# Causal attention by four heads and one query block instead of two heads and one or two query blocks: key ring, order of maxima, transposed gather

## What is computed

```python
x = x + 0.5 * ffn(layernorm(x))
x = x + attention(layernorm(x))
x = x + 0.5 * ffn(layernorm(x))
# ffn: weights of 4-bit codes times a scale per 32, H = 256, MLP_DIM = 2048
gate, up = xt @ Wg.T, xt @ Wu.T
out = (gelu_tanh(gate) * up) @ Wd.T
# attention, N_HEAD = 16, hd = 16
scores = einsum('bqhd,bkhd->bhqk', q, k) / sqrt(hd)
scores = where(causal, scores, finfo.min)
o = einsum('bhqk,bkhd->bqhd', softmax(scores), v)
return o @ Wo.T + bo
```

## Time and profile before

| | us |
|---|---|
| median of 3 runs (1113.87 to 1118.17) | 1116.4 |
| profiled execution, own time | 1118.69 |
| its span, first to last instruction | 1117.0 |
| attention, first score to last `weigh` | 351.8 to 829.3 |
| TensorE busy in the span | 1071.8 |
| VectorE busy | 699.0 |
| ScalarE busy | 577.9 |
| GpSimd busy | 112.6 |
| mean granted TensorE clock | 0.994 of 2.4 GHz |

### The profile page before, as it was taken

How to read it: one execution, slowest core, us unless ns; L and a number is a source line. 1 busy time by engine, 2 the same in 40 slices (tenths; PEclk the granted TensorE clock), 3 DMA queues, 4 the chain that set the end, 5 groups by cost and what they waited for, 6 DMA issues and landing times.

```text
span 1117.0 us, 17563 instructions
## 1 busy us (share of the span) xinstructions
PE 1071.8 (96%) x6448; PEld 707.1 (63%) x6448; DVE 699.0 (63%) x1620; ACT 577.9 (52%) x1107; POOL 112.6 (10%) x409
## 2 busy tenths in 40 slices
PE   4999999998999989999999999999999999999998
PEld 3888888887876533333333333333349888888887
DVE  5986545446556487888888888888544434344333
ACT  4764443342344656666777776777663333333322
POOL 1000000000001136331111111111100000000000
PEclk9999999998999899999999999999999999999999
DMA  6001040060030732322022202200000000000000
GB/s 195 2 1 47 7 126 1 11 175 16 10 123 1 202 65 55 67 53 53 14 41 54 53 1 54 53 1 2 1 1 1 1 20 1 1 19 1 20 1 19
DMA packets 75223, 43.81 MB, mean 39 GB/s; under 512 B 47161, under 2 KB 68993, under 8 KB 75137
## 3 DMA queue, kind: packets, MB, share of 16 engines
q1 hardware_dynamic: 75137, 42.68, 15.7%
HBM read 25.63 MB, written 16.78 MB: 38 GB/s over the span
## 4 chain that ended last, share of the span: by engine, by line
PE 87%; DVE 6%; ACT 2%; issue 2%; DMA 1%; SPq 0%; POOL 0%; ACTq 0%; DVEq 0%; POOLq 0%
PE psum L850 16%; PE psum L635 14%; PE psum L782 12%; PE psum L723 11%; PE psum L738 10%; PE psum L867 8%; PE psum L650 8%; DVE attn_part_max L1327 2%; PE psum L792 2%; PE psum L682 2%; ACT attn_prob L1141 1%; PE psum L826 1%; PE psum L694 1%; PE psum L124 1%; DVE attn_junk L1330 1%
## 5 line engine op out<-in xcount | busy, mean ns | idle before, releaser
L1141 ACT ACTIVATE attn_prob<-psum 128x512 f32<-128x512 f32 (+3 forms) x640 | 301.2, 540 | 145.7 <-PE psum L723 142.0
L1327 DVE TENSOR_REDUCE attn_part_max<-psum 128x1 f32<-128x512 f32 x384 | 243.7, 684 | 50.1 <-PE psum L738 48.2
L635 PE MATMUL psum<-ffn_xt,all_w_hi 128*128 128x512 f32 x512 | 166.0, 406 | 0.0
L782 PE MATMUL psum<-attn_prob,attn_vals 128*32 128x512 f32 (+3 forms) x1280 | 156.9, 544 | 0.1
L1330 DVE CUSTOM_DVE_ANT_0 attn_junk<-psum,attn_mask 128x128 bf16<-128x128 f32 (+3 forms) x256 | 116.9, 485 | 24.9 <-PE psum L738 24.4
L1432 DVE TENSOR_TENSOR ffn_act_out<-ffn_act_out,psum 128x512 f32<-128x512 f32 x64 | 44.0, 688 | 109.3 <-ACT ffn_act_out L1177 109.2
L650 PE MATMUL psum<-all_w_hi,ffn_inner 128*128 128x256 f32 x512 | 105.0, 288 | 0.1
L1177 ACT ACTIVATE ffn_act_out<-psum 128x512 f32<-128x512 f32 x64 | 38.2, 597 | 127.3 <-PE psum L850 127.3
L635 PEld LDWEIGHTS psum<-ffn_xt,all_w_hi 128*128 128x128 f32 x512 | 92.7, 192 | 16.4 <-issue 0.3
L867 PE MATMUL psum<-all_w_hi,ffn_inner 128*128 128x256 f32 x512 | 102.5, 283 | 0.1
L635 PE MATMUL psum<-ffn_xt,all_w_lo 128*128 128x512 f32 x256 | 100.7, 393 | 0.0
(11 more groups left out here) (150 smaller groups left out, 1674.2 us busy)
## 6 DMA issues: line engine op xcount, KB each, us to landing
qk_rows<-qkv_parts SPq DMA_DIRECT2D x16, 384.0 KB, 2.5
qk_rows<-qkv_parts SPq DMA_DIRECT2D x16, 256.0 KB, 2.9
attn_q_early<-qk_rows SPq DMA_DIRECT2D x8, 384.0 KB, 4.5
attn_q_late<-qk_rows SPq DMA_DIRECT2D x8, 384.0 KB, 3.7
attn_k_mid<-qk_rows SPq DMA_DIRECT2D x3, 768.0 KB, 6.7
attn_k_late<-qk_rows SPq DMA_DIRECT2D x3, 768.0 KB, 7.3
all_x<-in_L_attn_h SPq DMA_DIRECT2D x4, 512.0 KB, 6.7
v_rows<-qkv_rows_v SPq DMA_DIRECT2D x16, 128.0 KB, 2.5
```

The costliest lines, as they stand in the source:

```text
L635: last = nc.tensor.matmul(psum[:, 2 * m + q % 2, :], w_part[a][:, 3 * g + m, pl, o:o + P], xt[:, b % 2, c, pl, :], start=(n == 0), stop=(n ...
L782: last = nc.tensor.matmul(psum[r:r + 32, O0, at:BT], vals[:, k0 * SUB + kb + k, 2 * hd:2 * hd + 32], prob[:, (4 * d + 2 * k + hd) % PRING, ...
L1141: nc.scalar.activation(prob[:, n % PRING, at:BT], psum[:, S0 + n % SBANKS, at:BT], ACT.Exp).then_inc(s["exp"], 1)
L1327: nc.vector.tensor_reduce(to, psum[:, bank, :], AX.X, ALU.max).then_inc(s["max_read"], 1)
```

## The change

A group is now one query block and four heads, so 16 groups take the place of 32. A step is four heads by one key block; 160 steps stay. The accumulator holds one head in each 32 rows and `gather` becomes four 128x128 transposes; `normalise` picks each head's columns from the turned tile. Keys and values lie in a ring of six chunks of 512 keys, each loaded by itself when the step is done that frees its slot, queries in four slots. The maxima go chunk by chunk of keys (c outside, i inside), always four heads at a time. `max_row` issues four DMAs, one per head. `turn_max` turns 48 rows instead of 24. Two groups instead of four are prepared in the last feed-forward block, with the same 48 maxima. The score of the first group of each pair of heads no longer covers the first 128 queries of the second key block, which were masked.

```diff
 QSLOTS = 4
-KSLOTS = 12
-LOADS = 3
+KSLOTS = 6
+NHQ = 4
 SBANKS = 3
 MBANKS = 3
 PRING = 8
-VW = 34
+VW = 67
+VALUES_AT = (0, 2, 33, 35)
...
-            groups = [(qt, p) for half in range(2) for p in range(NPAIR) for qt in (2 * half, 2 * half + 1)]
+            groups = [(qt, u) for half in range(2) for u in range(NH // NHQ) for qt in (2 * half, 2 * half + 1)]
             NG_A = len(groups)
-            steps = [(g, kb) for g, (qt, _) in enumerate(groups) for kb in range(0, SUB * (qt + 1), 2)]
+            steps = [(g, kb) for g, (qt, _) in enumerate(groups) for kb in range(SUB * (qt + 1))]
...
-            chunks = [(g, i, c) for g, (qt, _) in enumerate(groups) for i in range(SUB) for c in range(qt + 1)]
-            EARLY = 4
-            N_EARLY = 2 * sum(1 for g, _, _ in chunks if g < EARLY)
+            loads = [(n, c) for n in range(NG_A // 2) for c in range(groups[2 * n + 1][0] + 1)]
+
+            def key_load(g, c):
+
+                return loads.index((g // 2, c))
+
+            def keys_free(r):
+
+                if r < KSLOTS:
+                    return 8
+                n, c = loads[r - KSLOTS]
+                return begin[2 * n + 1] + SUB * (c + 1)
+
+            def queries_free(g):
+
+                return begin[g - QSLOTS + 1]
+
+            chunks = [(g, i, c) for g, (qt, _) in enumerate(groups) for c in range(qt + 1) for i in range(SUB)]
+            EARLY = 2
+            N_EARLY = NHQ * sum(1 for g, _, _ in chunks if g < EARLY)
-                return 0 if d < 9 else 4 * (d - 8) if d < 12 else 12 + (d - 11) * 84 // 36 if d < 48 else 96 + 2 * (d - 47)
+                return 0 if d < 9 else 2 * d - 14 if d < 14 else 12 + (d - 13) * 5 // 4 if d < 45 else d + 7
...
+                at = [-2] * (N_EARLY // NHQ)
+                for n, (g, _, c) in enumerate(chunks[N_EARLY // NHQ:]):
+                    d = next(d for d in range(NS) if quota(d) > n)
+                    ready = [keys_free(key_load(g, c)) + 4] if key_load(g, c) >= KSLOTS else []
+                    ready += [queries_free(g) + 4] if g >= QSLOTS else []
+                    at.append(max([d, at[-1]] + ready))
...
-            turn_at = [-2, -2, -2, 1] + [chunk_at[ends[g]] + 2 for g in range(EARLY, NG_A)]
+            turn_at = [-2, 1] + [chunk_at[ends[g]] + 2 for g in range(EARLY, NG_A)]
...
-                        def load(n):
-
-                            qt, p = groups[2 * n]
-                            b, k0, cols = n % QSLOTS, slot[n], (qt + 2) * BT
-                            sp.dma_start(queries(b)[0:KR, :, :], qk_dram[0, 2 * p:2 * p + 2, :, qt * BT:cols].rearrange("h r t -> r h t")
-                                         ).then_inc(s[f"stack{b}"], 16)
-                            sp.dma_start(keys(k0)[0:KR, :, 0:qt + 2, :].rearrange("p a c t -> p a (c t)"),
-                                         qk_dram[1, 2 * p:2 * p + 2, :, 0:cols].rearrange("h r t -> r h t")).then_inc(s[f"stack{b}"], 16)
-                            sp.dma_start(vals[:, k0 * SUB:(k0 + qt + 2) * SUB, 1:1 + 2 * HD], v_dram[p, :, 0:SUB * (qt + 2), :]
-                                         ).then_inc(s[f"stack{b}"], 16)
+                        def load_queries(g):
+                            qt, u = groups[g]
+                            sp.dma_start(queries(g)[0:KR], qk_dram[0, NHQ * u:NHQ * (u + 1), :, qt * BT:(qt + 1) * BT].rearrange("h r t -> r h t")
+                                         ).then_inc(s[f"q_in{g % QSLOTS}"], 16)
+
+                        def load_keys(r):
+
+                            n, c = loads[r]
+                            u, k = groups[2 * n][1], r % KSLOTS
+                            sp.dma_start(keys(r)[0:KR], qk_dram[1, NHQ * u:NHQ * (u + 1), :, c * BT:(c + 1) * BT].rearrange("h r t -> r h t")
+                                         ).then_inc(s[f"kv_in{k}"], 16)
+                            for h in range(2):
+                                at = 1 + VW // 2 * h
+                                sp.dma_start(vals[:, k * SUB:(k + 1) * SUB, at:at + 2 * HD], v_dram[2 * u + h, :, c * SUB:(c + 1) * SUB, :]
+                                             ).then_inc(s[f"kv_in{k}"], 16)
                         def max_row(g):
                             sp.wait_ge(s["max_rows"], g + 1)
-                            b, o = g // 2 % QSLOTS, g % 2 * BT
-                            for hd in range(2):
-                                sp.dma_start(queries(b)[KR:KR + NPART, hd, o:o + BT], max_rows[NPART * SUB * hd:NPART * SUB * (hd + 1), g % 2, :]
+                            for hd in range(NHQ):
+                                sp.dma_start(queries(g)[KR:KR + NPART, hd, :], max_rows[NPART * SUB * hd:NPART * SUB * (hd + 1), g % 2, :]
                                              ).then_inc(s[f"max_in{g % 4}"], 16)
...
-                            for n in range(4, NL):
-                                if free_at(n) == d:
-                                    sp.wait_ge(s["weighted"], begin[2 * before[n] + 2])
-                                    load(n)
+                            for g in range(QSLOTS, NG_A):
+                                if queries_free(g) == d:
+                                    sp.wait_ge(s["weighted"], d)
+                                    load_queries(g)
+                            for r in range(4, len(loads)):
+                                if keys_free(r) == d:
+                                    sp.wait_ge(s["weighted"], d)
+                                    load_keys(r)
...
                             g, kb = steps[d]
-                            qt, k0 = groups[g][0], slot[g // 2]
+                            qt, r = groups[g][0], key_load(g, kb // SUB)
+                            at = first_query(qt, kb)
...
-                            for hd in range(2):
-                                for k in range(2):
-                                    at = first_query(qt, kb + k)
-                                    r = 32 * (2 * hd + k)
-                                    last = nc.tensor.matmul(psum[r:r + 32, O0, at:BT],
-                                                            vals[:, k0 * SUB + kb + k, 2 * hd:2 * hd + 32],
-                                                            prob[:, (4 * d + 2 * k + hd) % PRING, at:BT], start=(kb == 0),
-                                                            stop=(kb == SUB * (qt + 1) - 2), skip_group_check=True)
+                            for hd in range(NHQ):
+                                last = nc.tensor.matmul(psum[32 * hd:32 * hd + 32, O0, at:BT],
+                                                        vals[:, r % KSLOTS * SUB + kb % SUB, VALUES_AT[hd]:VALUES_AT[hd] + 32],
+                                                        prob[:, (4 * d + hd) % PRING, at:BT], start=(kb == 0),
+                                                        stop=(kb == SUB * (qt + 1) - 1), skip_group_check=True)
                             last.then_inc(s["weighted"], 1)
                         def gather(g):
                             pe.wait_ge(s["o_copied"], g + 1)
                             pe.wait_ge(s["x_free"], gather_use[g])
                             for i in range(SUB):
-                                last = nc.tensor.matmul(psum[:, X0, i * VW:(i + 1) * VW], o_sb[:, g % 2, i * P:(i + 1) * P], pick[:, :],
-                                                        start=True, stop=True)
+                                last = nc.tensor.transpose(psum[:, X0, i * P:(i + 1) * P], o_sb[:, g % 2, i * P:(i + 1) * P], ident[:, :])
...
```

184 lines of the change are left out of this document (74 added, 110 removed).

## The result

The changed kernel takes 1140.6 us (median of 4 runs, 1138.3 to 1143.9); the kernel before took 1117.3 beside it (median of 4, 1113.9 to 1122.3). The ratio is 1.0207, 95% interval 1.0158 to 1.0256: slower, by 2%. The prediction was 1134, with a range of 1116 to 1150 and 0.80 on slower. The profiled execution of the changed kernel took 1139.0, with a span of 1137.3; the span before was 1117.0. So 20.3 us are to be explained, where the prediction's sum had 17.3.

A forecast was written before the change was run, and what follows sets the result against it. TensorE was taken to bound the kernel, with VectorE and ScalarE within 30%. Step terms of +12.3 and +5 for the clock made +17.3: 1136.0 for the profiled execution, 1134 for the median, range 1116 to 1150.

The forecast's parts named there:

- The clock: Behind waiting steps: 6.4 us at half speed, some 2.5 us lost each, two falls in five; +5, bounds 0 and +15.
- steps 9 to 11: Early attention: narrow maxima and normalisation, then a waiting step of 5.8 us; 17.6 us against 14.3, +3.3.
- steps 12 to 47: Attention: ten steps with eight maxima 48.1, the other 26 64.4, step 15's wait 3.3; 117.8 us against 114.2, +3.6.
- the cycles: Steps 48 to 131, three cycles of 28 steps: 80.9 us each against 78.5, +7.2 for three.
- rival 1: Clock falls at every wait, six times 2.5 us instead of two: 1144, up to 1149; chance 0.16.
- The wait: Steps 11, 15, 59, 87, 115, 143: score waits for four row DMAs, 5.05 us instead of 1.7 to 2.5.
- VectorE takes it back: Diagonal steps and the one behind: VectorE needs 2.4 to 2.5 us where TensorE needs 1.8 to 2.6; 2.5 counted.
- The lump: In the later part, behind two steps without maxima, a step with twelve narrow maxima: 4.1 us.
- Steps 132 to 158: End of the attention: gains of two narrow steps and two gathers less the wait at 143 (+3.2), -1.5.
- TensorE's 27 us: Attention: gathers (25.9 to 8.8 us), fewer turns (about -3) and diagonal steps (-7) take about 27 us off TensorE.
- The ring: Key chunks land late by 1 to 2 us in steps 68, 96 and 124: 1139; chance 0.12.
- Lag of VectorE: VectorE makes up its lag in full steps, so TensorE's gain stays: 1107, chance 0.06; half of it, 1116 to 1126, 0.12.

The follow-up runs named there:

- the last run: Changed kernel with one DMA per row, key loads 5 and 6 behind group 2's row, maxima three steps behind key requests, six turns earlier: 1109.3 us, ratio 0.993.

## Why the prediction came out right, and where it was wrong

The direction and the mechanism held: the row of maxima, four issues on one queue, one step ahead. The number, 1134 against 1140.6, owes much to errors that cancel, which is luck. The clock is parted off by the run with products in the wait: the changed kernel is 12.9 us longer than it in steps 12 to 158. So the sum of +17.3 was off by +7.9 for the clock (12.9 instead of 5), +5.5 in steps 9 to 11, +0.7 at the end, and by -4.4 ahead of the attention, -1.8 in steps 0 to 8, -3.2 in steps 12 to 47, -1.5 in the cycles and -0.1 in the steps behind: together, before rounding, +3.0, which makes the 20.3 that were measured. The two largest errors alone would have put it at 1147; and the measured time lies nearer to the 1144 of rival 1 than to the forecast.

- **The wait.** Predicted 5.05 us and about 16 us in all; steps 15, 59, 87, 115, 143 took 4.9 to 5.1. The runs with one, two and four issues (step 87: 3.24, 3.61, 5.06) show that issues pay for it.
- **The clock: the step that failed most.** I counted "two falls in five", +5. Half clock came with all four late waits and with both early ones; holding it up gave 14.6 us. Rival 1 was right in rate. Its price of 2.5 us was a little high: behind 59, 87, 115 and 143 the steps took 1.6, 1.6, 3.2 and 1.9 us too much. The argument against it, that a waiting step still has 1.9 us of work where the gap of the earlier trace rows had 0.37, did not hold. The section "HAM oscillation" of the Trainium skill's page TensorE: Matmul & The Clock Gate describes a kernel with a wait for DMA of some 3 to 5 us in each round, whose clock falls again in each round. The traces here agree, with gaps a little shorter or as long, 2.8 to 3.1 us (12 of 12 late waits in three kernels with four issues). Behind gaps of 0.95 to 1.14 us no fall is seen (0 of 12, four kernels with one issue), behind those of 1.3 to 1.6 us a fall in half the cases (4 of 8, with one issue or two).
- **Steps 9 to 11.** Predicted +3.3, measured +8.8. Step 11 took 10.49 us here, 9.22 and 6.92 in two other runs with the same SP queue, and 5.30 with the loads behind the row: so 1.6 to 5.2 us are the loads ahead of it, 5.2 in this execution. The prediction counted the row's own issues on SP and not the loads queued ahead of it. It looked at each queue by step; in time SP was late and still held loads of step 8 at step 11. Its 5.8 us for that step were right for a queue without them, where it took 5.30.
- **Steps 12 to 47.** Predicted +3.6 without the clock; with the clock held 114.6 against 114.2, so +0.4, and the rest of the +4.9 is the clock. The count of the steps themselves was close, 115.8 against 114.6. The 2 us added to it for what the same count misses in the kernel before came to nothing, and the rest of the error is the count's own 1.2.
- **The cycles.** Predicted 80.9 without the clock; with it held, 80.4. The rest up to 82.0 to 83.6 is the clock. The sum was nearly right, its label was not: the six steps counted at VectorE's 2.5 us, 15.0, took 14.1 (in the second cycle 76, 86, 88 and 101 to 103, with the clock held), one of them (103) 2.18 us beside four full reductions, just under the 2.2 that the prediction named as a sign of being wrong. "VectorE takes it back" does not hold here, as the halved reductions show. The lump took 4.86 us instead of 4.1, which offset most of this. What takes back TensorE's gain in a cycle are the wait (2.6 us in the changed kernel: 5.06, where the last run has 2.12 and 0.37 in the step before) and the lump.
- **Steps 132 to 158.** -1.5 predicted, 75.6 against 77.2 with the clock held: -1.6. The clock turned it into +0.5.
- **Ahead of the attention.** I took no change; it was -4.4. Most of this goes with one piece at half clock and not with the change. The same stretch before and after:

```profile
265.00:280.00 15.00, 11.96 (x55) 9.22 (x54) 10.40 (x29) 3.78 (x6) 0.61 (x4) 0.77 0.00 1
```

```profile
265.00:280.00 15.00, 12.26 (x65) 8.80 (x63) 14.08 (x41) 5.66 (x8) 0.84 (x4) 1.00 0.00 1
```

Where the clock of this stretch is 1.00 (six profiles of the changed order) the attention starts at 346.5 to 347.4; where it is 0.89 (six others) at 347.6 to 349.9, and so does the kernel before with halved reductions, at 349.5; where it is 0.77, in the profile before, at 351.8. Why the clock falls there in one execution and not in another was not tried.
- **TensorE's 27 us.** The gathers gave more than their 17 (four transposes 0.44, not 0.55: 32 x 0.81 - 16 x 0.44 = 18.9). But TensorE's busy time in the last run is 1053.0, against 1071.8 before: 18.8 less, not 27. About 9 us reach the median (1118.2 to 1109.3) once waits and clock are mostly out of the way.
- **The other rivals.** The ring was not late at four steps: no maximum waited for keys. At three steps neither, at two by 1 to 2 us. The page Perfetto Trace Analysis of the Trainium skill, "DMA Optimizations", had spoken for this rival, since it holds DMAs of under 2 KB to be costly. No run here shows such a cost, though none was made for it: a key load of 384 KB in pieces of 2 KB landed 5.0 to 5.8 us after its issue before, the same 384 KB in pieces of 1 KB after 4.2 to 4.4 now, and values of 64 KB after 3.7, sooner than the 5.4 and 7.9 of the larger loads. The slowest of them before, and the same tile after:

```profile
attn_k_mid<-qk_rows SPq DMA_DIRECT2D x2, 384.0 KB, 5.8
```

```profile
attn_k_mid<-qk_rows SPq DMA_DIRECT2D x8, 384.0 KB, 4.2
```

Lag of VectorE did not absorb anything that decides, and the waits were there.

## What to carry to other kernels

When groups get larger, ask for each transfer between two groups how many DMAs it is now, on which queue, and what is queued ahead of them in time, not in steps; a layout in the destination's order can make one DMA of four. Price a wait of TensorE twice, once as idle time and once at half clock behind it, and look for short gaps rather than few. A transfer can be started sooner by moving only its producer's last link; to move all the work ahead of it may run into the next limit, as the keys did.
